# Offset convolution read from on-chip memory, row weights made pair by pair beside it, with GpSimd making the weights' low halves

## The reference

```
x   = wm @ (x - mean) + beta                 # whitening, wm from 10 Newton steps
om  = conv3x3(x, w_off) + b_off              # 27 planes
py, px = om[:9] + row + ky, om[9:18] + column + kx
s   = bilinear(x, py, px) * sigmoid(om[18:]) # zero outside the image
out = relu(batch_norm(einsum(s, w) + b)) + x
```

## Time and profile before

| | us |
|---|---|
| median of 3 runs | 2315.51 |
| lowest and highest run | 2312.31, 2316.44 |
| profiled execution, its own time | 2317.37 |
| its span from first to last instruction | 2315.2 |

### The profile page before, as it was taken

How to read it: one execution, slowest core, us unless ns; L and a number is a source line. 1 busy time by engine, 2 the same in 40 slices (tenths; PEclk the granted TensorE clock), 3 DMA queues, 4 the chain that set the end, 5 groups by cost and what they waited for, 6 DMA issues and landing times. The chain is left out here.

```text
span 2315.2 us, 62313 instructions
## 1 busy us (share of the span) xinstructions
PE 1634.0 (71%) x24206; PEld 1092.1 (47%) x24207; DVE 1592.1 (69%) x2182; ACT 1454.3 (63%) x2219; POOL 611.2 (26%) x1168
## 2 busy tenths in 40 slices
PE   4756980000008999999999999999999999990620
PEld 4532330000006666666666666666666666660310
DVE  5343006656717898898898898998998899993205
ACT  2211224343217898898898898998998899980102
POOL 2000000000033444444444443434444444430000
PEclk9788995555557999999999999999999999995555
DMA  2177874667675766666667766666667666640008
GB/s 117 33 189 187 237 216 157 214 235 277 219 228 118 163 145 157 155 150 147 162 141 153 162 146 142 167 148 154 159 150 151 156 148 160 152 98 23 3 0 341
DMA packets 288863, 362.22 MB, mean 156 GB/s; under 512 B 61852, under 2 KB 260819, under 8 KB 285013
## 3 DMA queue, kind: packets, MB, share of 16 engines
q1 hardware_dynamic: 209552, 226.57, 38.8%
q0 software_dynamic: 36864, 59.94, 11.6%
q10 hardware_dynamic: 42182, 72.05, 9.1%
HBM read 253.94 MB, written 104.39 MB: 155 GB/s over the span
## 5 line engine op out<-in xcount | busy, mean ns | idle before, releaser
L758 POOL DMA_DIRECT2D rows<-scratch_parts x1152 | 587.5, 518 | 799.5 <-PE ps_even_y L790 777.3
L799 PE MATMUL ps_odd_y<-rows,sel 32*128 32x504 f32 (+2 forms) x928 | 465.3, 501 | 362.6 <-DMA rows<-scratch_parts 348.8
L942 DVE TENSOR_TENSOR G<-odd_y,ps_odd_v 128x504 f32<-128x504 f32 (+2 forms) x928 | 571.9, 658 | 127.7 <-PE ps_odd_v L820 85.7
L820 PE MATMUL ps_odd_v<-tent_x,stage 32*128 32x171 f32 (+1 forms) x5568 | 654.5, 329 | 0.0
L890 ACT COPY odd_y<-ps_odd_y 128x504 f32<-128x504 f32 (+2 forms) x928 | 527.7, 569 | 117.2 <-PE ps_odd_y L799 99.1
L820 PE MATMUL ps_even_v<-tent_x,stage 32*128 32x171 f32 (+3 forms) x5568 | 552.8, 329 | 37.8 <-ACT even_v L896 29.3
L951 DVE TENSOR_TENSOR G<-even_v,ps_even_y 128x1008 f32<-128x1008 f32 (+2 forms) x464 | 539.4, 1163 | 22.8 <-ACT even_v L896 22.6
L820 PEld LDWEIGHTS ps_odd_v<-tent_x,stage 32*128 32x128 f32 x5568 | 515.8, 189 | 0.0
L820 PEld LDWEIGHTS ps_even_v<-tent_x,stage 32*128 32x128 f32 x5568 | 429.2, 189 | 182.4 <-issue 168.7
L838 PE MATMUL ps_r<-G,conv_w 128*32 128x224 f32 (+1 forms) x8832 | 483.4, 346 | 9.8 <-ACT res L901 9.8
L896 ACT COPY even_v<-ps_even_v 128x1008 f32<-128x1008 f32 (+2 forms) x464 | 450.5, 971 | 23.5 <-PE ps_odd_v L820 15.8
(11 more groups left out here) (134 smaller groups left out, 951.8 us busy)
## 6 DMA issues: line engine op xcount, KB each, us to landing
place<-scratch_px SPq DMA_DIRECT2D x960, 105.0 KB, 3.5
scratch_parts<-parts ACTq DMA_DIRECT2D x18, 3136.0 KB, 16.9
rows<-scratch_parts POOLq DMA_DIRECT2D x960, 52.5 KB, 3.5
x<-scratch_xh SPq DMA_DIRECT2D x48, 406.0 KB, 6.3
place<-scratch_px SPq DMA_DIRECT2D x192, 84.0 KB, 2.9
scratch_om<-om ACTq DMA_DIRECT2D x64, 196.0 KB, 7.0
rows<-scratch_parts POOLq DMA_DIRECT2D x192, 42.0 KB, 2.8
scratch_conv<-res SPq DMA_DIRECT2D x448, 14.0 KB, 1.9
```

The costliest lines, as they stand in the source:

```text
L758: pool.dma_start(bass.AP(tensor=rows[b][:].tensor, offset=32 * g * pitch + here, ap=[[2 * pitch, Y_KINDS], [GROUP * W, 3], [1, count * W]] ...
L799: nc.tensor.matmul(ps_odd_y[:, lo:hi], sel[32 * g:32 * g + 32, :], taps(rows, 32 * g, 32, p, lo, hi), start=True, stop=True).then_inc(odd_ ...
L820: m = nc.tensor.matmul(sub(ps_v[g // 2], 0, 128, i * 512 + lo + first, dims), stage[32 * g:32 * g + 32, j * IMAGE + v * C:j * IMAGE + (v + ...
L942: nc.vector.tensor_tensor(sub(G, 0, 128, slot(v) + i * ROW + lo, [[1, hi - lo]]), odd_y[p % 3][:, i * ROW + lo:i * ROW + hi], ps_v[1][:, i ...
```

## The change

- `XH` stays in SBUF and the offset convolution reads it there, 32 partitions (two images) at a time for a group of 8 images, with 9 taps of K=32 in place of 3 of K=128. DVE evacuates PSUM with bias and column pattern added, so that the plane of column offsets holds the places themselves; `px` is gone, `place` is loaded from `om`. `om` keeps 27 planes, even image rows ahead of odd ones.
- The row weights are made per pair of images, 126 partitions x 448 elements, in the same block as the convolution. POOL issues the loads and makes the low halves in place, ACT stores the halves with one DMA each.
- Ranges are taken by DVE from the evacuated planes, once for each group, by unit in place of by row.
- The clears of `stage` and `rows` move to the first block, the loads of the loop's constants to the whitening block, and the first loads of `stage`, `place` and `rows` into the new block.
- Behind the loop two loads gather the ranges in runs of 7 numbers.

The core of the diff, mostly its added side:

```diff
-PLANE = B * KK * HW
-OM_IMG = 32 * HW
-DENSE = PLANE // 128
-DCH = 784
-CHUNKS = DENSE // DCH
-RANGES = ("oy_max", "oy_min", "ox_max", "ox_min")
+PX, OY, MASK = range(3)
+PLANES = 3 * KK
+OM_IMG = PLANES * HW
+DCH = 448
+DENSE = 2 * KK * HW // DCH
+RANGES = ("max", "min")
...
+        def load_place(eng, pair, n):
+            b = n % 2
+            for i, g, here, there, count in row_sources(n):
+                eng.dma_start(sub(place[b], 32 * g, 32, here, [[GROUP * W, 3], [1, count * W]]),
+                              dram("om", (pair * 2 + i) * OM_IMG + PX * KK * HW + there, [[0, 32], [HW, 3], [1, count * W]])
+                              ).then_inc(place_loaded[b], 16)
...
+        def load_stage(eng, pair, c):
+            first, count = BANDS[c]
+            for j, (x0, lo, hi) in enumerate(COLUMNS):
+                for g in (0, 2, 1, 3):
+                    eng.dma_start(sub(stage, 32 * g + lo - x0, hi - lo, j * IMAGE + first * C, [[1, count * C]]),
+                                  dram("xt", ((pair * 2 + g % 2) * W + lo) * XT_ROW + (TOP - 5 + first) * C,
+                                       [[XT_ROW, hi - lo], [1, count * C]])).then_inc(stage_loaded[c], 16)
...
-                pool.memset(XH[:, :], 0.0).then_inc(zeroed, 1)
-                pool.memset(zeros[:, :], 0.0).then_inc(zeroed, 1)
-                pool.wait_ge(zeroed, 2)
+                cleared = [tile[:, :] for tile in (XH, zeros, stage)] + [tile[:, :].bitcast(fp32) for tile in rows]
+                for tile in cleared:
+                    pool.memset(tile, 0.0).then_inc(zeroed, 1)
+                pool.wait_ge(zeroed, len(cleared))
...
+            tent_y = [sb(f"tent_y{i}", WIN * DCH, parts=DENSE) for i in range(3)]
+            high = [sb(f"high{i}", WIN * DCH, f32r, parts=DENSE) for i in range(2)]
...
+                for tile, name in ((woff, "woff"), (boff, "boff"), (pattern, "pattern")):
+                    n = tile[:].shape[1]
+                    sp.dma_start(tile[:, :], dram(name, 0, [[n, 128], [1, n]])).then_inc(w_loaded, 16)
+                sp.dma_start(shift[:, :], dram("shift", 0, [[WIN, 128], [1, WIN]])).then_inc(grid_loaded, 16)
+                for c in range(len(BANDS)):
+                    load_stage(sp, 0, c)
+                for g in range(GROUPS):
+                    sp.wait_ge(evacuated, NCH * (g + 1))
+                    for q in range(PER_GROUP):
+                        for j in range(4):
+                            h, i = j // 2, j % 2
+                            sp.dma_start(dram("om", (g * GB + 2 * q + i) * OM_IMG + h * OM // 2,
+                                              [[HW, PLANES], [HW // 2, 2], [1, OM // 2]]),
+                                         sub(om, 32 * j, PLANES, q * OM, [[OM // 2, 2], [1, OM // 2]])).then_inc(om_stored, 16)
+                    if g == 0:
+                        sp.wait_ge(om_stored, 64 * PER_GROUP)
+                        load_place(sp, 0, 0)
+                sp.wait_ge(ranged, GROUPS)
...
+                def load_dense(pair):
+                    b = pair % 2
+                    pool.wait_ge(om_stored, 64 * PER_GROUP * (pair // PER_GROUP + 1))
+                    wait(pool, distant, pair - 1)
+                    wait(pool, scaled, pair - 1)
+                    for tile, kind in ((mask[b], MASK), (oy[b], OY)):
+                        pool.dma_start(tile[:, :], dram("om", pair * 2 * OM_IMG + kind * KK * HW,
+                                                        [[OM_IMG, 2], [DCH, DENSE // 2], [1, DCH]])).then_inc(loaded[b], 16)
+                load_dense(0)
+                load_dense(1)
+                for pair in range(PAIRS):
+                    t = tent_y[pair % 3]
+                    pool.wait_ge(high_ready, pair + 1)
+                    nc.gpsimd.tensor_tensor(t[:, :].bitcast(f32r), t[:, :], high[pair % 2][:, :].bitcast(fp32),
+                                            ALU.subtract).then_inc(low_ready, 1)
+                    if pair + 2 < PAIRS:
+                        load_dense(pair + 2)
+                    if pair == 2:
+                        pool.wait_ge(high_stored[0], 16)
+                        pool.wait_ge(low_stored[0], 16)
+                        load_rows(pool, 0, 0)
...
+                        top = ch // 2 + 2 * ROWS * (ch % 2)
+                        for k in range(KK):
+                            for q in range(PER_GROUP):
+                                for h in range(2):
+                                    m = nc.tensor.matmul(ps_o[n % 2][64 * h:64 * h + 64, q * 512:q * 512 + CH],
+                                                         woff[32 * q:32 * q + 32, k * 64:(k + 1) * 64],
+                                                         sub(XH, 32 * q, 32, g * PADHW + (h * HALF + top + k // 3) * PADW + k % 3,
+                                                             [[2 * PADW, ROWS], [1, W]]),
+                                                         start=(k == 0), stop=(k == KK - 1))
...
-                    nc.scalar.activation(sorted_rows(mask[b]), by_parity(logit[b]), ACT.Sigmoid).then_inc(masked, 1)
+                    act.wait_ge(loaded[b], 32 * (n // 2 + 1))
+                    wait(act, low_stored[n % 3], 16 * (n // 3))
...
+                    nc.scalar.copy(kinds(high[b]), kinds(tent_y[n % 3])).then_inc(high_ready, 1)
...
+                    where = [[DCH, DENSE], [B * KK * HW, WIN], [1, DCH]]
+                    act.wait_ge(high_ready, n + 1)
+                    act.dma_start(dram("parts", n * 2 * KK * HW, where), kinds(high[n % 2]).bitcast(fp32)
+                                  ).then_inc(high_stored[n % 2], 16)
+                    act.wait_ge(low_ready, n + 1)
+                    act.dma_start(dram("parts", (WIN * B + n * 2) * KK * HW, where), kinds(tent_y[n % 3])
+                                  ).then_inc(low_stored[n % 3], 16)
...
+                def evacuate(g, ch):
+                    n = g * NCH + ch
+                    dve.wait_ge(convolved, n + 1)
+                    wait(dve, om_stored, 64 * PER_GROUP * g)
+                    nc.vector.tensor_tensor(sub(om, 0, 128, ch * CH, [[OM, PER_GROUP], [W, ROWS], [1, W]]),
+                                            sub(ps_o[n % 2], 0, 128, 0, [[512, PER_GROUP], [W, ROWS], [1, W]]),
+                                            sub(pattern, 0, 128, 0, [[0, PER_GROUP], [0, ROWS], [1, W]]),
+                                            ALU.add).then_inc(evacuated, 1)
...
+                for ch in range(NCH):
+                    evacuate(0, ch)
+                take_ranges(0)
+                for n in range(PAIRS):
+                    t = tent_y[n % 3]
                     dve.wait_ge(distant, n + 1)
+                    nc.vector.tensor_scalar(t[:, :], t[:, :], 1.0, 1.0, ALU.min, ALU.subtract).then_inc(capped, 1)
                     dve.wait_ge(capped, n + 1)
                     dve.wait_ge(masked, n + 1)
+                    nc.vector.tensor_tensor(kinds(t), kinds(t), sub(mask[n % 2], 0, DENSE, 0, [[0, WIN], [1, DCH]]),
+                                            ALU.mult).then_inc(scaled, 1)
+                    g, at = n // PER_GROUP + 1, n % PER_GROUP
+                    if g < GROUPS and at < 2:
+                        evacuate(g, 2 * at)
+                        evacuate(g, 2 * at + 1)
+                    if g < GROUPS and at == 2:
+                        take_ranges(g)
...
+                    sp.dma_start(sub(ranges, 0, PAIRS, k * 128 * HALF_UNITS, [[HALF_UNITS, 128], [1, HALF_UNITS]]),
+                                 dram(name, 0, [[HALF_UNITS, PAIRS], [PAIRS * HALF_UNITS, 128], [1, HALF_UNITS]])
+                                 ).then_inc(S["x_ranges"], 16)
```

More of the change, by code:

```diff
@@ L115, in program @@
         wm = sb("wm", 128)
-        zeros = sb("zeros", XT_ROWS * C)
+        zeros = sb("zeros", NEAR * C)
+        IMAGE = VIEW_ROWS * C
+        sel32, sel = sb("sel32", 128), sb("sel", 128, f32r)
+        conv_w, conv_b, at = sb("conv_w", KK * 32), sb("conv_b", 1), sb("at", 1)
+        stage = sb("stage", len(COLUMNS) * IMAGE)
+        rows = [sb(f"rows{b}", KK * GROUP * W, f32r) for b in range(2)]
+        place = [sb("place0", KK * GROUP * W)]
+        dcn_loaded = sem("dcn_loaded")
+        BANDS = ((0, 16), (16, 16), (32, 16), (48, VIEW_ROWS - 48))
@@ new lines, in load_place, with load_rows @@
+        def load_place(eng, pair, n):
[4 more added lines that the diff above has]
+                              ).then_inc(place_loaded[b], 16)
+        def load_rows(eng, pair, n):
+            b = n % 2
+            pitch = rows[b][:].ap[0][0]
+            for i, g, here, there, count in row_sources(n):
+                eng.dma_start(bass.AP(tensor=rows[b][:].tensor, offset=32 * g * pitch + here,
+                                      ap=[[2 * pitch, Y_KINDS], [GROUP * W, 3], [1, count * W]]).bitcast(fp32),
```

(28 more changed lines are left out.)

297 lines of the change are left out of this document (96 added, 201 removed).

## The result

The median is 2393.7 us (2380.7 to 2397.6, 4 runs) against 2313.9 (2305.5 to 2316.4, 4 runs) of before: ratio 1.034, 95% interval 1.029 to 1.039. 2262 was forecast, and the range ended at 2342.

What follows compares the result with a forecast made beforehand. It took a ring of uncovered loads, front, cap and multiplication, and POOL's subtraction, 25.0 us a pair, to bound the weight stage. 2317.4 - 58.4 + 4.5 = 2263.5 us profiled, median 2262, range 2195 to 2342.

Steps and rivals of the forecast that it cites:

- Loads: Pair's offset loads, asked for when POOL's subtraction ends, uncovered: 5.8 us a pair, upper end 11.5.
- the second: Rival: the queue of stores, not bytes, sets the loads; 5.7 us more a pair, 80 in all, 2342 us; 15%.
- The 14 turns: Weight stage: fourteen pairs in a ring at 25.0 us each, from first low halves at 265 to 615.4.
- the front: ScalarE's nine instructions from the sigmoid on, at 448 elements, ahead of the high copy: 5.2 us a pair.
- copy and subtraction: Cap and multiplication beside the copy, in turn with POOL's subtraction: 5.8 us, then 7.8 (6.2 to 9.3).
- The start-up: From the block's start at 196 us through stage loads, offset stores and first pairs to first low halves: 265.4.
- From the last turn to the first sample: After 615.4 us: last pair to 627.3, its store to 636.8, then cast, distance and cap 2.6, so 639.4.
- The loop: Sampling loop, claimed still 1394 us long; a move of more than 10 us was a sign of being wrong.
- Behind the loop: Range loads in short runs against shorter reductions: +4.5 us, between -2 and +13.
- the terms of POOL and VectorE: Per pair: cap 1.95 and multiplication 3.8 on VectorE, then POOL's subtraction 7.8, the two in turn.
- The first rival: POOL and VectorE run side by side: a pair takes 22.3 us, 38 less in all, 2224 us; 22%.
- the third: Rival: POOL's subtraction costs more than three streams; at twice the value 109 us more, 2371 us; 8%.

Runs made afterwards that it cites:

- e4: Against the changed kernel, ScalarE issues a pair's low store only behind the next front (sigmoid and distances); 2322.4 us, ratio 1.001 to the kernel before.
- e1: Against the changed kernel, a pair's two loads are cut into four of 63 partitions each; 2314.0 us, ratio 0.995 to the kernel before.
- e5: Against the changed kernel, four loads of 63 partitions and the late low store together; 2256.7 us, ratio 0.971 to the kernel before.
- e2: Against the changed kernel, POOL issues the loads of pair n+2 ahead of the subtraction of pair n; 2261.4 us, ratio 0.973 to the kernel before.
- e7: Against the changed kernel, loads of 63 partitions, late low store, subtraction on VectorE, loads issued after a pair's product; 2178.7 us, ratio 0.939 to the kernel before.
- e9: Against e7, evacuations and ranges of the next group one pair earlier; 2191.8 us, ratio 0.944 to the kernel before.

## Why the prediction was wrong

The step that failed is "Loads": "The part above 2.3, scaled by 441/1176, gives 5.8". It scaled by bytes a time that few engines set, and it read the old loads (11.5 us beside stores, 6.0 without) as bandwidth. The measured 12.9 lies above even the upper end of 11.5. What the runs showed in its place: 8.6 us for these loads on four engines with no store beside them (e4), 9.0 for four loads of 63 partitions beside the store (e1), 3.9 with neither (e5). Of the rivals it was the second, to which I gave 15%, with the mechanism of its last sentences and more than its price: 107 us against 80. The sentence that I set against it, that there were less than half the bytes, was the error itself: fewer bytes, but in two loads on two engines each.

The sum, from the profiled run (2397.6 against 2263.5 forecast, 134.1 apart):

- The 14 turns: 457.1 against 350, +107.1. Of a plain turn of 31.4 us the loads are 7.1 over, the front 0.25 under, copy and subtraction as forecast; two turns in which a group's offsets are stored take 36.5 and 36.7.
- The start-up, to the first low halves: 285.1 against 265.4, +19.7. In the timeline:

```profile
226.62 1.79 DVE L607 TENSOR_TENSOR om<-ps_o,pattern 128x1568 f32<-128x1568 f32 x1 [4.18 <-PE ps_o L555]
228.43 14.31 SPq L503 DMA_DIRECT2D scratch_om<-om  x16
...
246.09 0.97 POOL L528 DMA_DIRECT2D mask<-scratch_om  x1 [139.24 <-DMA scratch_om<-om]
...
259.83 1.28 ACT L570 ACT_TABLE_LOAD   x1 [73.12 <-DMA oy<-scratch_om]
```

  The stores start 8.3 us late, behind the convolution: chunks stand 6.0 us apart (the four evacuations start at 208.76 to 226.62), at a granted clock of 1.00 (2.4 GHz) from 206 us on, after a mean of 0.63 from 200 to 206 us, in which the matmuls began. I had counted the rows as matmuls; each matmul stands in two rows (the profile has 2304 for the 1152 of this convolution), so 36 sets cost 24 us, not 12. The stores and their landing are 1.2 over, the four loads take 13.7 in place of 5.8 (7.5 in e1), the rest is 2.3, of which 1.9 is POOL's first subtraction beside a cap.
- From the last turn to the first sample: -3.2.
- The loop: 1407.0 from first sample to ranges, +13.0, which is more than the 10 us that the prediction named as a sign of being wrong. In the ten experiments, whose loops have the same instructions, it is 1392.9 to 1403.2, with busy TensorE from 1332.6 to 1339.6; so the change isn't shown to lengthen it, and what the few us above that are stays open.
- Behind the loop: +2.0 in place of +4.5.

Right were the terms of POOL and VectorE. Its subtraction takes 7.73 alone, 7.8 forecast, and it starts at the copy's end but runs only from the end of the multiplication:

```profile
275.45 9.66 POOL L535 TENSOR_TENSOR tent_y<-tent_y,high 126x3584 fp32r<-126x3584 f32 x1 [25.89 <-ACT high L580]
275.46 2.02 DVE L627 TENSOR_SCALAR tent_y<-tent_y 126x3584 f32<-126x3584 f32 x1
277.51 11.34 DVE L630 TENSOR_TENSOR tent_y<-tent_y,mask 126x3584 f32<-126x3584 f32 x1
...
745.87 7.73 POOL L535 TENSOR_TENSOR tent_y<-tent_y,high 126x3584 fp32r<-126x3584 f32 x1 [3.70 <-ACT high L580]
```

The last row is without VectorE beside it. The 9.66 of the first are 1.9 more, beside a cap of 2.02. In a plain pair the multiplication ends 2.8 us after POOL's instruction starts, and 2.8 + 7.6 = 10.4. In the first pair POOL comes first, and the multiplication waits: it ends at 288.85, 3.74 after POOL, its usual 3.89 taking 11.34. That is what the Trainium skill says (SBUF — State Buffer, section Who interferes with whom), and e2 fits it. The first rival is thereby excluded, and the third, a costlier subtraction.

## What to carry to other kernels

A load's time is read from the engines that it occupies: here 441 KB on four engines, at some 23 GB/s each, are 5 us by estimate, to which the issues, the landing and a store issued in the same moment come; bytes over the bandwidth of all engines is the wrong scale for a load whose outermost dimension is 2. Ahead of moving work to another engine, ask what the ring waits for: here neither VectorE nor POOL was the bound, and POOL's slower subtraction only lengthened a chain whose longest link was an uncovered load. With that link shortened (e7: four loads, a late store, the subtraction back on VectorE) the same design beats both kernels, 2179 us against 2314 and 2394.

## What was not expected of the hardware

- Two loads of 220 KB with a slowest dimension of 2 ran at 90 GB/s on a DMA share of 0.24, with nothing else in flight; beside a store of 1764 KB they needed 12.9 us in place of 8.6.
- An issue of POOL took 0.82 us for the load of 2 x 63 runs and 0.52 for one of 63 (1.03 for two).
- SP's 16 stores of offsets took 14.3 us to issue in the start-up, 31.1 to 32.2 (2.0 each) at a boundary of e7 and 39.6 at one of e9.
